# An attention and expert kernel on one core: weighted rows are stored and gathered by token instead of being added into sums, in three groups of batches instead of two

## The reference

```
q, k, v = heads(x @ w.T + b)           # 16 heads of 16, rotary on q and k
att = softmax(mask(q k^T / 4)); y = att @ v
x = layernorm(x + y @ wp.T + bp)
probs = softmax(x @ gate_w.T)          # 32 experts
top_w, top_idx = top_k(probs, 8);  top_w /= sum(top_w)
out = sum over the 8 chosen experts e of  top_w[e] * (u * silu(g)) @ down_w[e].T,   g, u = split(x @ gate_up_w[e].T)
x = layernorm(x + out)
```

## Time and profile before

| | before |
|---|---|
| median of three runs | 2736.49 us |
| the profiled execution, its own time | 2743.34 us |
| its span in the profile | 2741.5 us |
| busy PE / DVE / ACT / POOL | 2022.8 / 1589.0 / 1396.8 / 1605.0 us |
| granted TensorE clock, mean | 0.898 |

### The profile page before, as it was taken

The page is one execution under the profiler, slowest core; times in us unless marked ns, Lnnn a source line. Parts: engine busy times, 40 slices in busy tenths (PEclk is TensorE's granted clock), DMA queues, the critical chain, the costliest instruction groups (busy, mean ns, idle before and its releaser), DMA issues.

```text
span 2741.5 us, 52019 instructions
## 1 busy us (share of the span) xinstructions
PE 2022.8 (74%) x16429; PEld 1369.6 (50%) x16429; DVE 1589.0 (58%) x3300; ACT 1396.8 (51%) x2801; POOL 1605.0 (59%) x1252
## 2 busy tenths in 40 slices
PE   3888888888888888878876765677777776776740
PEld 2444544444544444444465654556655565665630
DVE  3767767776767676675533442333334343776768
ACT  1465565565654454544554543455555554665630
POOL 0005334554334554334478888888888888888880
PEclk8899999999998998899888988899999998998975
DMA  4466677776676666569478887889999888999996
GB/s 131 127 205 215 200 240 234 246 248 205 210 233 221 226 228 190 190 195 315 155 191 162 151 147 143 150 153 179 193 192 191 153 152 168 256 256 249 245 196 193
DMA packets 388340, 543.77 MB, mean 198 GB/s; under 512 B 47536, under 2 KB 283344, under 8 KB 387024
## 3 DMA queue, kind: packets, MB, share of 16 engines
q1 hardware_dynamic: 241200, 333.53, 39.9%
q0 software_dynamic: 121344, 178.33, 33.4%
q10 hardware_dynamic: 25536, 28.58, 3.2%
HBM read 257.95 MB, written 301.55 MB: 204 GB/s over the span
## 4 chain that ended last, share of the span: by engine, by line
POOL 27%; PE 22%; issue 20%; DVE 12%; DMA 12%; ACT 4%; SPq 3%; ACTq 0%; DVEq 0%; POOLq 0%
POOL y_sum L735 24%; PE ps L854 4%; PE ps L913 3%; DMA qk_parts<-pbuf 3%; PE ps L879 3%; POOL x_sorted L724 3%; PE ps L901 3%; DVE mn L1453 3%; SPq L562 2%; PE ps L799 2%; DMA ks<-qk_parts 1%; PE ps L865 1%; DVE qf L1426 1%; PE ps L926 1%; PE ps L881 1%
## 5 line engine op out<-in xcount | busy, mean ns | idle before, releaser
L1113 ACT ACTIVATE pT<-ps 128x1024 f16<-128x1024 f16 (+4 forms) x1344 | 755.1, 576 | 715.2 <-PE ps L903 352.9
L724 POOL DMA_INDIRECT x_sorted<-xhl,idx x512 | 534.5, 1044 | 384.0 <-DVE xhl L1524 232.2
L1453 DVE TENSOR_REDUCE mn<-ps 128x1 f32<-128x512 f32 (+3 forms) x704 | 421.1, 635 | 81.4 <-PE ps L881 75.3
L967 PE MATMUL ps<-pT,gu_hi 128*128 128x256 f16 x1280 | 368.4, 288 | 13.2 <-issue 12.9
L968 PE MATMUL ps<-pT,gu_hi 128*128 128x256 f16 x1280 | 368.4, 288 | 0.0
L969 PE MATMUL ps<-pT,gu_lo 128*128 128x256 f16 x1280 | 368.3, 288 | 0.0
L879 PE MATMUL ps<-ks,qs 96*128 96x512 bf16 (+3 forms) x1024 | 295.9, 322 | 80.3 <-DVE mn L1453 35.1
L901 PE MATMUL ps<-qs,ks 99*128 99x512 bf16 (+3 forms) x1024 | 312.0, 319 | 4.8 <-DMA qs<-mrow 3.5
L1027 PE MATMUL ps<-dn,vx 128*128 x640 | 184.6, 288 | 121.9 <-DVE vx L1616 63.3
L903 PE MATMUL ps<-maskk,identb 128*128 128x128 bf16 x1024 | 234.3, 230 | 0.0
L1610 DVE SCALAR_TENSOR_TENSOR vx<-vx,ps 128x512 f32<-128x512 f32 x160 | 110.0, 688 | 187.9 <-PE ps L969 182.5
(11 more groups left out here) (221 smaller groups left out, 4344.6 us busy)
## 6 DMA issues: line engine op xcount, KB each, us to landing
y_sum<-zero SPq DMA_DIRECT2D x136, 256.0 KB
qs<-x_sorted SPq DMA_DIRECT2D x115, 296.0 KB, 3.9
ks<-x_sorted SPq DMA_DIRECT2D x115, 296.0 KB, 3.8
qk_parts<-pbuf SPq DMA_DIRECT2D x64, 384.0 KB
qs<-qk_parts SPq DMA_DIRECT2D x64, 384.0 KB, 4.0
ks<-qk_parts SPq DMA_DIRECT2D x64, 384.0 KB, 5.2
x_sorted<-zeros_h SPq DMA_DIRECT2D x66, 296.0 KB
qk_parts<-pbuf SPq DMA_DIRECT2D x64, 256.0 KB
```

Source lines behind the costliest of these rows:

```text
L724: pool.indirect_dma_start(xsort[g][:, :], bass.IndirectOffsetOnAxis(ap=at, axis=0), xhl_rows[:, t, :], None).then_inc(s_scat, 16)
L967: mmul(o, w_hi[k], x_hi[k], start=k == 0, stop=False)
L1113: return nc.scalar.activation(o, i, f, **k)
L1453: V.tensor_reduce(mn[:, tt, h0:h0 + nh], ps[:, odd_bank("max", at, m), 0:nh * n].rearrange("p (a n) -> p a n", a=nh), axis=AX.X, op=ALU.ma ...
```

## The change

The adding DMAs, the sums in DRAM, the zero fills and the token numbers in the rows are gone. SP stores each weighted block with an ordinary DMA (`block_out`) at its own place in a table `y_sorted` that has the layout of `x_sorted`. When a group is finished, POOL gathers for each tile of 128 tokens the 8 rows of every token (`gather`, 8 indirect DMAs of 128 rows, 512 in all), with the same `idx` as the scatter, into one of three buffers `yg`, which lie where the attention stacks were. DVE adds the eight rows in three steps of 1024, 512 and 256 elements. The groups are now batches 0 to 7, 8 to 12 and 13 to 15, with 80 + 56 + 40 = 176 slots, since each group may fill up its experts' last blocks. The tiles stand at steps 84 to 136 (32 tiles), 140 to 176 (20) and from 180 (12). `ysb` has four buffers in place of six, and ACT does both blocks' `rows_copy` from slot 82. Blocks from number 136 on have ten places to land in, before that fourteen.

In stage one the 32 scatters of a batch are spread over the steps from e = 30 to e = 24 of the next batch but one, one or two a step, and POOL waits before each until the first score of that step is done.

```
-GROUPS = ((0, 12), (12, 16))
+GROUPS = ((0, 8), (8, 13), (13, 16))
-TILES = [(SLOT0[g + 1] + 5, SLOT0[g + 2] + 3) for g in range(NG - 1)] + [(S + 6, S + 10)]
+TILES = [(SLOT0[g + 1] + 4, SLOT0[g + 2] + 2) for g in range(NG - 1)] + [(S + 4, S + 16)]
-NYR = 6
+NYR = 4
+NYG = 3
+SCATTER_FIRST, SCATTER_STEPS = 30, 27
+            step = (b + 1) * STEPS + SCATTER_FIRST + n * SCATTER_STEPS // (NT * TOPK)
...
+            def block_out(n):
+                wait(sp, s_yc[n % NYR], 2 * (n // NYR + 1))
+                dst = ysort[GROUP_OF[n // 2]][bass.ds(y_row(n), BLK), :].rearrange("(p m) c -> p m c", m=2)
+                sp.dma_start(dst, ysb[n % NYR].bitcast(I32)).then_inc(s_ys[n % NYR], 16)
...
+            def at_step(i, e):
+                if i < NB:
+                    wait(pool, s_st, 64 * i + 2 * e + 1)
+                else:
+                    wait(pool, s_g, (i - NB) * STEPS + e - 1)
...
+            def gather(q):
+                b, t, r = q // NT, q % NT, q % NYG
+                g = batch_group(b)
+                if q == 0:
+                    for k in range(NYR):
+                        wait(pool, s_yc[k], 2 * (2 * SLOT0[1] // NYR))
+                if q == GROUPS[g][0] * NT:
+                    for k in range(NYR):
+                        wait(pool, s_ys[k], 16 * (2 * SLOT0[g + 1] // NYR))
+                wait(pool, s_cmb, 7 * (q - NYG) + 3)
                 for k in range(TOPK):
                     at = idx[:, b, t * TOPK + k:t * TOPK + k + 1]
+                    pool.indirect_dma_start(yg[:, r, k, :].bitcast(I32), None, ysort[g][:, :],
+                                            bass.IndirectOffsetOnAxis(ap=at, axis=0)).then_inc(s_yg[r], 16)
-            def add_rows(n):
-                wait(pool, s_yc[r], 2 * (n // NYR + 1))
-                wait(pool, s_add[j], 32 * (n // NJ))
-                for m in range(2):
-                    pool.indirect_dma_start(yacc[GROUP_OF[n // 2]][j][:, :], bass.IndirectOffsetOnAxis(ap=xid[n % NXR][:, m, :], axis=0),
-                                            ysb[r][:, m, :], None, compute_op=ALU.add).then_inc(s_add[j], 16)
...
             def rows_copy(n):
-                    wait(act, s_add[(n - NYR) % NJ], 32 * ((n - NYR) // NJ + 1))
+                    wait(act, s_ys[n % NYR], 16 * (n // NYR))
...
             def total(q):
+                wait(dve, s_yg[q % NYG], 16 * TOPK * (q // NYG + 1))
+                V.tensor_tensor(rows[:, 0:4, :], rows[:, 0:4, :], rows[:, 4:8, :], ALU.add).then_inc(s_cmb, 1)
+                V.tensor_tensor(rows[:, 0:2, :], rows[:, 0:2, :], rows[:, 2:4, :], ALU.add).then_inc(s_cmb, 1)
+                V.tensor_tensor(a, rows[:, 0, :], rows[:, 1, :], ALU.add).then_inc(s_cmb, 1)
-                V.tensor_reduce(a, acc[q % NACC].rearrange("p j c -> p c j"), axis=AX.X, op=ALU.add).then_inc(s_cmb, 1)
```

More of the change, by code:

```diff
@@ L107, in plan, with scatter_plan, uses_before @@
     return tiles_at
-TILES_AT = plan()
-RA = [(hi - lo) * T + BLK for lo, hi in GROUPS]
-FILLS = [(g, j, n) for g in range(NG) for j in range(NJ) for n in range(RA[g] // (2 * P))]
+SCATTER_FIRST, SCATTER_STEPS = 30, 27
+def scatter_plan():
+    at = {}
+    for b in range(B):
+        for n in range(NT * TOPK):
+            step = (b + 1) * STEPS + SCATTER_FIRST + n * SCATTER_STEPS // (NT * TOPK)
+            at.setdefault(divmod(step, STEPS), []).append((b, n))
+    return at
+SCATTER_AT = scatter_plan()
+TILES_AT = plan()
+LATER = 2 * (SLOT0[1] - 12)
+EARLY_HOMES, LATE_HOMES = list(range(14)), list(range(10, 20))
+HOMES = [EARLY_HOMES[n % 14] if n < LATER else LATE_HOMES[(n - LATER) % 10] for n in range(2 * S)]
+NXR = 20
+def uses_before(n):
+    return [k for k in range(n) if HOMES[k] == HOMES[n]]
 GROUP_OF = [g for g in range(NG) for _ in range(NSLOT[g])]
@@ L222, in build @@
     xsort = [nc.dram_tensor(f"x_sorted{k}", [NROW[k], RW // 2], I32, kind="Internal").ap() for k in range(NG)]
-    yacc = [[nc.dram_tensor(f"y_sum{k}_{j}", [RA[k], C], F32, kind="Internal").ap() for j in range(NJ)] for k in range(NG)]
+    ysort = [nc.dram_tensor(f"y_sorted{k}", [NROW[k], C], I32, kind="Internal").ap() for k in range(NG)]
     with ExitStack() as ctx:
@@ L264, in build @@
         base0 = [route[:, 2 + g * E:2 + (g + 1) * E] for g in range(NG)]
-        qs = sb("qs", [P, 3, 4, T], BF16)
-        ks = sb("ks", [P, 3, 4, T], BF16)
+        stacks = sb("stacks", [P, 2, 3, 4, T], BF16)
+        qs, ks = (stacks[:, n, :, :, :] for n in range(2))
         vx = sb("vx", [P, 2 * VW])
@@ L575, in clear_tail @@
                 sp.dma_start(xsort[g][bass.ds(row, BLK), :].rearrange("(a b) c -> a (b c)", a=16),
[L576 to L584, removed]
+                             zeros_h.rearrange("(a b) c -> a (b c)", a=16)).then_inc(s_tail, 16)
             def block_in(n):
@@ L761, in routing @@
                     store_x1(i - 1)
-                if e == 29 and has(i, 1, NB):
-                    scatter(i - 1, 0)
+                for b, n in SCATTER_AT.get((i, e), ()):
+                    at_step(i, e)
+                    scatter(b, n)
             for i in range(NB):
@@ L767, in _ @@
                     routing(i, e)
-            for k in range(NK + 2):
+            for k in range(2 * STEPS):
                 routing(NB + k // STEPS, k % STEPS)
-                if ADD_LAG <= k < S + ADD_LAG:
-                    for a in range(2):
-                        add_rows(2 * (k - ADD_LAG) + a)
-                for q in TILES_AT.get(k - 2, ()):
-                    if q % NT == NT - 1:
-                        last_rsqrt(q // NT)
+            for q in range(B * NT):
+                gather(q)
+                if q > NT and q % NT == 1:
+                    last_rsqrt(q // NT - 1)
+            last_rsqrt(B - 1)
         @block.tensor
@@ L1348, in _ @@
             V.memset(mhalf[:, :], -0.5).then_inc(s_set, 1)
-            V.memset(zero[:, :], 0.0).then_inc(s_set, 1)
-            V.memset(xhl[:, :, :], 0.0).then_inc(s_set, 1)
             V.memset(mk[:, 0:NT, :], 0.0).then_inc(s_set, 1)
```

140 lines of the change are left out of this document (58 added, 82 removed).

## The result

The changed kernel takes 2542.99 us (median of four executions, 2538.61 to 2556.6), the kernel before 2735.47 on the same chip. The ratio is 0.9302, with a 95% interval from 0.9271 to 0.9334: 192 us less, where 148 were predicted. The prediction had 2588 and a range of 2525 to 2680. The profiled execution is the longest of the changed kernel's, 2556.6 us with a span of 2554.8; the forecast for that span was 2592.

A forecast was written before the change was run, and what follows sets the result against it. Stage two was taken as bound by POOL's issue of adding DMAs. First gather at 1840, plus 346 to 2186, second group from 2205, third from 2449, end 2592; span 2594, time 2588 us, 8-in-10 range 2525 to 2680.

The forecast's parts named there:

- Stage one, "+20 - 15 = +5 us": Stage one: 20 us added by ACT's wait at upper_rows, 15 us gained from removed zero fills and stretched scatters.
- Slots 0 to 82, "5.25 and 12 us": Stage two's slots without tiles: 5.25 us a slot, plus 12 us for the end of batch 15.
- The gather's price, 1.044 + 0.30: POOL in stage two: a gather costs the plain scatter's mean 1.044 us plus 0.30 of issue, 1.34.
- the 7% rival: Stage two: a gather costs POOL what an add costs, 15.3 us a tile, time 2828; chance 7%.
- Group one, "346 us, slots at 6.4": First group's 32 tiles, from step 84: POOL is the bound, needing 346 us, with slots at 6.4 us.
- Group two, "15 us, then 19 at 11.2, and two slots": Second group: first tile 15 us after 2205, 19 more at 11.2 us, last rows copied two slots on, landed at 2449.
- The tail: Third group after 2449: twelve tiles at 10.8 us, 130 us, then 4.5 of landing and 9.0 to the end, 2592.
- The DMA engines as the bound, 17%: Rival: DMA engines bound the slots with tiles, 7.2 us a slot and 6.9 in group two, time 2652; chance 17%.
- Everything at its best, 18%: Case: slots at 5.08, gathers at 0.97, stage one no slower; span 2515, time 2510; chance 18%.
- From the span to the time: Whole kernel: span 2594, and the profiled execution before was 6.9 us above the median, so the time was put at 2588.

The follow-up runs named there:

- the second experiment: The kernel before with the addition taken out of its 640 indirect DMAs, so they store rows plainly: 2403.75 us.
- the first: The changed kernel with 4 of the 8 gathers of each tile, DVE adding as many elements as before: 2388.07 us.
- the third: The changed kernel with the two groups of before, (0, 12) and (12, 16): 2653.49 us.
- the run with 20 steps: The changed kernel with each batch's scatters spread over 20 steps in place of 27: 2544.31 us, ratio 0.93 to the kernel before.

## Why the prediction was right, and where it was off

The mechanism was right: POOL's issue of adding DMAs bound stage two (the second experiment), gathers are cheaper for it and still bind the slots with tiles (the first), and the groups decide when they start (the third). The time lies in the stated range, but 7 us under the forecast's own narrower one of 2550 to 2625. The sizes, by the prediction's own points in the profiled span:

| point | predicted us | trace us | difference so far | this step's |
|---|---|---|---|---|
| first slot | 1393.5 | 1380.9 | -12.6 | -12.6 |
| slot 82 | 1836 | 1815.3 | -20.7 | -8.1 |
| first gather | 1840 | 1820.4 | -19.6 | +1.1 |
| second group's first gather | 2205 | 2187.5 | -17.5 | +2.1 |
| third group's first gather | 2449 | 2418.4 | -30.6 | -13.1 |
| end | 2592 | 2554.8 | -37.2 | -6.6 |

*Stage one, "+20 - 15 = +5 us".* The step that failed most, together with the second group. The wait of ACT exists, as said, and is 9.4 us in 9 times, not 20; and it is not on the path, as the run with 20 steps shows. Part of that is the landing of a scatter: I took 5 us and said that no row shows it, but in the trace of before it is 3.9 us by the median. What the missing zero fills give is small too: the DMA share falls from 0.68 to 0.62 in 100 to 1360 us, but the wait for `qk_parts` is no shorter (21.1 against 18.6), and only that for `attention` is (5.2 against 17.2). The 7.5 us by which the first slot is earlier than before (1380.90 against 1388.45) are within what executions differ: with the smaller first group, which leaves stage one's work as it is, the first slot was another 16 us earlier. In the six experiments on the changed kernel it stood at 1359.4 to 1371.9, so the changed kernel's own profile has the latest of seven; but the kernel before with plain DMAs, where stage one is untouched, had it at 1369.6. Nothing can be made of a term of 5 us there.

*Slots 0 to 82, "5.25 and 12 us".* 434.4 us against 442.5. The first 32 slots took 175.1 in place of 180, the other 50 took 259.3 in place of 262.5: the 12 us for the end of batch 15 and the 5.25 a slot were both a little too much.

*The gather's price, 1.044 + 0.30.* 1.020 + 0.30. The plain scatter was the right neighbour, and the 7% rival, which needed 1.39, is out. The mean hides that most gathers take 0.95 in every group: in the first, 45 of 256 take more than 1.05 us, the longest 1.86, and the mean is 1.03; in the second, 27 of 160, with the same mean; in the third 10 of 96, with a mean of 0.97. DVE is busy 68% of the time in the first two and 39% in the third. The power operation took 1.05 us in place of 1.62. The Trainium skill, SBUF — State Buffer, the trap "DVE blocks DMA", says that descriptors can't be written from POOL while DVE runs in a mode that takes both ports; by that and these rows it would cost a gather an estimated 0.08 us on average here at most (1.03 against 0.95). The direction agrees; no row shows which mode DVE ran in, and the stretches differ in what else the DMA engines carry, so the cause of the long ones is open.

*Group one, "346 us, slots at 6.4".* 348.7 us and 6.65. Right: 54 steps at 5.3 would be 286 us, and the tiles take longer.

*Group two, "15 us, then 19 at 11.2, and two slots".* The chain of the changed kernel from the last gather of this group to the third group's (start, length, what):

```profile
2404.89 4.62 DMA stacks<-y_sorted,idx
...
2412.44 0.43 DVE x1T L1665
2412.89 0.33 SPq L636
...
2413.93 2.53 DMA y_sorted<-yev
...
2416.61 1.76 issue
```

The last tile is there at 2409.5, 222.0 us after the group's first gather, where 227.8 were predicted: 10.93 us a tile and not 11.2. And from there to the next group's first gather it is 8.9 us, not 16: the last product ended at 2409.5 too, so only the copy and the store of the last rows were still to come, not two whole slots. What the 8.9 us were: by its timeline ACT had copied these rows by 2410.8, but in the chain, on SP, their store stands behind the load of a residual (L636), which waits for the tile's L1665 on DVE, and so it began at 2413.93. -5.8 and -7.1 make the 13.

*The tail.* Twelve tiles at 10.45 in place of 10.8, 125.4 us in place of the 130 of the sum; 11.0 us behind the last gather in place of 13. From the last product, at 2409.2, POOL, DMA and DVE are alone for 146 us; I had said about 130, and had counted only the gathers.

*The DMA engines as the bound, 17%.* They move 298 and 302 GB/s at a share of 0.92 and 0.93, above the 249 at 1.01 of before, so a full share with adds in it does not give the rate at which plain rows would fill them. The smaller first group moved 335 GB/s at 0.98 with PE busy 95%. The Trainium skill, DMA: Bandwidth & Descriptors, on where 436 GB/s comes from, puts a core's HBM limit at about 358 GB/s; the 335 stays under it. The highest slice of that kernel's page (its row of GB/s over 40 slices, below) is 356, just under it too, and there the share of the DMA engines was 1.00. Whether the smaller first group is close to being held by them no run tells.

```profile
GB/s 147 116 149 153 207 215 202 186 195 216 204 173 202 286 195 168 192 180 202 198 245 235 268 219 230 229 244 278 325 356 348 327 329 264 284 293 275 217 126 115
```

*Everything at its best, 18%.* 2515 for the span; the trace lies between it and the forecast, 40 above the one and 37 under the other. The slots (5.30, not 5.08) and the gathers (10.9, not 10.4) were on the forecast's side, stage one on the other.

*From the span to the time.* I took 6.9 us off because the profiled execution before was above its median. The profiled execution after was 13.6 above its own. With 6.9 off, 2594 gives 2587 and not the 2588 of the forecast, which took off 6. So the 45 us between forecast and median are 37.4 of the steps, less 6, and 13.6 of this. That the median lies further below the forecast than the trace did is a matter of which execution was profiled.

## What to carry to other kernels

Where an engine issues DMAs in a row, count issues times the time of one, and read that time for each form apart: an adding DMA by list costs POOL half as much again as a plain one, however well it is hidden at the DMA engines. Moving a sum from the DMA to an idle engine frees the issuer but makes it wait until all the rows are there, so the number and the sizes of the groups then matter much (97 us between two groups and three, by single profiles) and are worth runs of their own. And an edit that spreads work out is free only where the engine has idle time behind it: the same one cost 22 us where POOL was the bound and nothing where it wasn't.

## What the runs showed of the hardware that was not expected

- The adding itself costs POOL, not the addresses: 1.564 us on average with it, 1.002 without, for the same rows to the same places.
- With adds the DMA engines are at a share of 1.01 for 249 GB/s, with plain rows at 0.98 for 335 GB/s and, over 63 us, at 1.00 for 356, so a share near 1 does not say how much more they could carry.
- TensorE's granted clock is 1.00 (2.4 GHz) over whole stretches of 300 to 350 us where PE has hardly a gap (95% and 94% busy), and 0.94 on average in the changed kernel's first group at 82%, a mixture of the two levels of 1.2 and 2.4 GHz: here a bound on POOL went with some loss of PE's clock.
